# A transformer block with cross-attention on one core: the same instructions of the cross-attention stage in another order on all five engines

## The reference

```python
attn_in  = _adaln(x, cond, ln1_w, ln1_b, g1_w, g1_b, b1_w, b1_b)
x        = _attn(attn_in, attn_in, sa_wq, sa_wkv, sa_wo, sa_bo) + x      # self-attention
cross_in = _adaln(x, cond, ln1_w, ln1_b, g1_w, g1_b, b1_w, b1_b)
ctx_n    = _ln(context, ca_lnc_w, ca_lnc_b)
x        = _attn(cross_in, ctx_n, ca_wq, ca_wkv, ca_wo, ca_bo) + x       # cross-attention
ffn_in   = _adaln(x, cond, ln2_w, ln2_b, g2_w, g2_b, b2_w, b2_b)
x        = _gelu(ffn_in @ ff_w1 + ff_b1) @ ff_w2 + ff_b2 + x

def _attn(xq, ctx, wq, wkv, wo, bo):
    q = _rope(_heads(xq @ wq), sq, cq)                 # rotary embedding of queries
    k, v = split(ctx @ wkv); k = _rope(_heads(k), sk, ck)
    a = softmax(q @ k.T * DH ** -0.5)
    return (a @ v) @ wo + bo
```

## Time and profile before

| | us |
|---|---|
| median of 3 runs (lowest, highest) | 1930.57 (1927.43, 1931.12) |
| the profiled execution: its time, and its span | 1934.22, 1932.4 |

### The profile page before, as it was taken

The page is one execution under the profiler, slowest core; times in us unless marked ns, Lnnn a source line. Parts: engine busy times, 40 slices in busy tenths (PEclk is TensorE's granted clock), DMA queues, the critical chain, the costliest instruction groups (busy, mean ns, idle before and its releaser), DMA issues.

```text
span 1932.4 us, 54308 instructions
## 1 busy us (share of the span) xinstructions
PE 1871.5 (97%) x20617; PEld 1422.7 (74%) x20617; DVE 1480.6 (77%) x2316; ACT 978.1 (51%) x1732; POOL 1306.7 (68%) x859
## 2 busy tenths in 40 slices
PE   7999999978999999999999999999999999999999
PEld 4666767757777777777777777777777777777764
DVE  4999989966777777777777777777777777777741
ACT  3455555534655555455445545545554455445444
POOL 4878756514877777677777766777777678777661
PEclk8999999978999999999999999999999999999999
DMA  5332233211111111111111111111111111111100
GB/s 175 116 87 87 86 103 89 79 33 47 52 54 47 52 49 47 55 49 52 50 49 49 47 51 51 47 54 52 49 47 49 52 53 48 52 49 47 53 26 22
DMA packets 159899, 113.84 MB, mean 59 GB/s; under 512 B 80928, under 2 KB 123808, under 8 KB 159648
## 3 DMA queue, kind: packets, MB, share of 16 engines
q1 hardware_dynamic: 122784, 110.09, 17.5%
q10 hardware_dynamic: 36864, 0.28, 1.0%
HBM read 31.21 MB, written 1.05 MB: 17 GB/s over the span
## 4 chain that ended last, share of the span: by engine, by line
PE 81%; DVE 5%; issue 5%; DMA 4%; POOL 3%; ACT 1%; SPq 1%; ACTq 0%; DVEq 0%; POOLq 0%
PE S L1602 22%; PE OB L1616 19%; PE PB L1513 9%; PE PB L1518 7%; PE S L1583 6%; DMA swapped<-turned 3%; PE S L1385 2%; PE PB L1351 1%; PE S L1636 1%; PE S L1645 1%; PE S L1474 1%; PE S L1627 1%; PE OB L1413 1%; PE OB L1396 1%; POOL psum_acc L769 1%
## 5 line engine op out<-in xcount | busy, mean ns | idle before, releaser
L825 POOL TENSOR_TENSOR psum_acc<-psum_acc,P 124x1024 f32<-124x1024 f32 x256 | 611.3, 2388 | 117.1 <-ACT P L1002 97.8
L1002 ACT ACTIVATE P<-S 124x1024 f32<-124x1024 f32 (+1 forms) x448 | 432.7, 966 | 416.3 <-PE S L1602 416.0
L1223 DVE TENSOR_REDUCE mxc<-S 128x2 f32<-128x1024 f32 x384 | 470.1, 1224 | 152.4 <-PE S L1583 148.3
L1518 PE MATMUL PB<-wsplit,ctxH 64*124 64x256 f32 x1632 | 309.3, 279 | 0.0
L1602 PE MATMUL S<-QH,KH 64*124 64x256 f32 (+1 forms) x1664 | 299.9, 307 | 8.7 <-ACT P L1002 6.1
L1513 PE MATMUL PB<-ctxH,wsplit 64*128 64x512 f32 x1004 | 298.1, 376 | 3.3 <-issue 2.3
L1616 PE MATMUL OB<-P,V 124*64 124x256 f32 (+1 forms) x2236 | 296.3, 389 | 0.0
L1602 PE MATMUL S<-MX,share 64*124 64x256 f32 (+1 forms) x1664 | 275.6, 279 | 0.0
L1602 PE MATMUL S<-QL,KH 64*124 64x256 f32 (+1 forms) x1664 | 275.1, 278 | 0.0
L1602 PE MATMUL S<-QH,KL 64*124 64x256 f32 (+1 forms) x1664 | 275.0, 278 | 0.0
L1602 PEld LDWEIGHTS S<-QH,KH 64*124 64x124 f32 (+1 forms) x1664 | 206.6, 181 | 85.5 <-issue 61.3
(11 more groups left out here) (192 smaller groups left out, 4078.3 us busy)
## 6 DMA issues: line engine op xcount, KB each, us to landing
swapped<-turned SPq DMA_DIRECT2D x512, 128.0 KB, 2.0
kv_w<-sa_kv_dram SPq DMA_DIRECT2D x64, 128.0 KB, 2.3
qswapped<-qturned SPq DMA_DIRECT2D x128, 64.0 KB, 1.9
ctxT_all<-ctx_dram SPq DMA_DIRECT2D x8, 624.0 KB, 4.6
q_w<-sa_wq_dram SPq DMA_DIRECT2D x64, 64.0 KB, 2.0
q_w<-ca_wq_dram SPq DMA_DIRECT2D x64, 64.0 KB, 2.1
o_room<-ca_wo_dram SPq DMA_DIRECT2D x64, 64.0 KB, 2.1
swapped<-turned SPq DMA_DIRECT2D x128, 16.2 KB, 1.8
```

The source lines that it names most:

```text
L825: pool.tensor_tensor(acc, acc, P_of(J, c)[0:rows, :, 0:w], ALU.add).then_inc(x.acc, 1)
L1002: act.activation(P_of(J, c)[0:rows, :, 0:w], SP[0:rows, :, 0:w], ACT.Exp, scale=SCALE).then_inc(x.e, 1)
L1223: dve.tensor_reduce(mxc[:, t, :, c:c + 1], MP[:, :, 0:w], AX.X, ALU.max).then_inc(x.am, 1)
L1518: last_v = pe.matmul(out, context, weights, start=(not second and k == 0), stop=(second and k == len(values) - 1))
```

## The change

The instructions stay the same; their order changes on each engine. The diff of the two lines that show the notation (PE's first, and SP's):

```diff
@@ CROSS = Cross("ca", DC, M, 124, 512,
-                  "s4+-1 x0+1 a5 y0+1 s5+-1 a6 p3+-1 o+-2 p4+-1 s6+-1 x1+1 a0+1 y1+1 s0 n0 p5+-1 a1+1 n1 x2+1 s1 y2+1 a2+1  "
...
-                  "wo+1 k2+1 k3+1 w+4 i+-1 k0+2 q+2 r+5 k1+2")
+                  "s4+-1 x0+1 a5 y0+1 s5+-1 a6 p3+-1 p4+-1 o+-2 s6+-1 x1+1 a0+1 n0 y1+1 s0 a1+1 p5+-1 x2+1 n1 s1 y2+1 a2+1  "
...
+                  "k2+1 wo+2 r+5 k3+1 i+-1 w+4 k0+2 q+2 k1+2")
```

## The result

The kernel after takes 1940.66 us (median of 5 runs, 1938.58 to 1946.6), the kernel before 1930.57 (median of 5, 1927.43 to 1934.46): ratio 1.0058, with a 95% interval of 1.0035 to 1.0080 (a ratio here is made of all runs and isn't the quotient of the two medians). A second set of 11 runs of after gave 1.0032 (1.0017 to 1.0047). By the medians it is slower by 10.1 us in the first set and by 6.9 in the second; forecast were 9.7. Both profiled executions of after are shorter than their medians: 1939.39 us with a span of 1937.6, and a span of 1934.6.

The account below looks back on a forecast made before the run. The prediction took PE, busy 97% of the span, to bound the kernel. Its terms 5.9 + 3.3 + 1.3 - 0.8 gave +9.7 us, 1940.3 us on the median 1930.6, with a range of 1924 to 1949.

Parts of the forecast that it names:

- the main term: On DVE: with `ka3` ahead of `kl2`, late K copies delay PE's `x3`; 5.9 us plus 3.3 for copies covered today.
- Two of its own signs: If right, `x3` waits for `kl2` in ten to eighteen steps; if wrong, late copies are fewer than nine.
- `ka0` before `dv`: On DVE: if `ka0`'s copy is late `dv` waits too, but is due only at `o`; 0 us (-3 to +3).
- `a1` ahead of `p5`: On PE: `a1` would wait for `am0` after late chunk 1 copies, one step in ten; 1.3 us, 0 to 4.
- The tail: Last steps on PE: the mean `n0`, moved ahead of `s0`, fills an idle 0.78 us; -0.8 us.
- SP, ACT, POOL at 0: New orders on SP, ACT and POOL hold nothing up; 0 us, for ACT and POOL 0 to 2.
- its likeliest case: The forecast itself, chance 0.56: 1934 to 1947 us, from no covered late copies and no `a1` wait to both upper bounds.
- The rival of no change: K copies come sooner or meet fewer instruction loads, so the sum goes to about zero: 1931 us; chance 0.20.
- The rival of a faster kernel: In odd steps `am1` and `a2` come 0.3 us sooner with `a1` moved up: 9.3 us, total 1920.5; chance 0.17.
- The clock rival: PE's holes of 1.5 us in nine steps lower its clock to half: 14.5 us more, 1955 us; chance 0.07.

Follow-up runs that it names:

- a_sp: The kernel after with SP's string of before (`wo` ahead of `k2`, `w` right behind `k3`, `r` after `q`): ratio 1.0041 to before.
- a_all3: The kernel after with three edits undone (`kl2` ahead of `ka3`, `dv` ahead of `ka0`, `p5` ahead of `a1`): ratio 1.0002 to before.
- b_ka0: The kernel before with one edit alone, VectorE's `ka0` ahead of `dv`: ratio 1.0061 to before.
- b_pe: The kernel before with TensorE's string of after, except that `p5` stays ahead of `a1`: ratio 0.9995 to before.
- b_ka3: The kernel before with one edit alone, VectorE's `ka3` ahead of `kl2`: ratio 1.0067 to before.

## Why the prediction was right, and where only its sum was

**Right: what bounds it and what carries the loss.** PE does; quiet steps stayed as long within 0.1 us a pair; what counts is which late copies PE gets to feel. In all 14 traces, every single copy of K or Q and of the maxima that was late by over 0.4 us lay beside a load of instructions. The reverse holds too: of 840 copies of chunk 3, 243 had no load that began between 1.5 us before their issue and 3.5 behind it, and each of them landed within 0.02 us of the median. And the mechanism of the main term is in the rows: 1.50 us idle before `x3` where 1.5 was worked out.

**Wrong: the main term, +9.2 us, measured -1.** The step that failed is the count, late copies of the last chunk in 0.29 of the steps (17 or 18), taken over from before to after. That average may serve for a load that falls anywhere. But before, 20 and 23 of 59 were late, and after 7: the same change that made each cost more made them three times rarer. Alone on the old order the edit costs 13.2 us at its place, more than forecast; in the change it costs next to nothing. The prediction had named this as its first rival (loads fall elsewhere as words move), with 0.20, and expected the total to go to zero with it. Two of its own signs speak against the main term: `x3` waits in four and seven steps of the two traces, not in ten to eighteen, and the late copies are seven, fewer than nine.

**Wrong: `ka0` before `dv`, priced at 0 (-3 to +3 for all the rest of DVE), measured +3.9 at `a5` and more with it.** The sentence was "`dv` is due at `o`, behind `p4` now". It looked at who needs `dv`'s result, and not at who needs the room that `dv` reads. `a3`'s wait for `qc` had shown exactly such a wait, in the earlier trace rows, and the same function makes both.

**Too small: `a1` ahead of `p5`, +1.3, measured +4.0.** The price of one such step was nearly right (0.4 us by the starts, 6.8 us in 16 steps; 0.3 forecast). The number of steps was not: the forecast took one in ten, six of 60, and 16 and 11 were late. Chunk 1's late copies had risen from 15 to 22.

**The tail, -0.8, measured +1.5.** The hole was filled and 0.55 us were gained up to the next one. The clock took it back in these two traces, which says nothing of the change, since it does so as often with the old order.

**SP, ACT, POOL at 0:** `a_sp` and `a_all3`, which keeps the new ACT and POOL strings, bear it out. `MX` waits went down by some 1 us (the column `s6` to `s0`), which was not forecast.

So the forecast's 9.7 = 9.2 + 1.3 - 0.8 came out as -1 at `x3`, +3.9 at `a5`, +4.0 at `a1`, -1.1 at `s0`, some 2.4 in quiet steps (0.08 us a pair, 30 pairs) and +1.5 in the tail, 9.7 again. That the two sums meet is luck, and the last term is not the change's. Of these 9.7 the two pairs of spans show 5.2 and 5.8 us (1937.6 - 1932.4, 1934.6 - 1928.8), because the first of the 60 steps began 5.5 and 3.4 us sooner in the traces of after. Of that some 2.8 us lie ahead of the stage's first `q`, and 1.7 in its first three steps, which the table leaves out. It began as early in `b_ka0` and `b_pe`, and late in `a_sp` (474.4 us). Whether an edit is behind that, no run settles. The medians of the runs show 10.1 and 6.9. The sum is right by two couplings of the same kind that took the place of the one that was priced. The range held it for a better reason: it was wide for the number of late copies. (By its own terms its likeliest case reaches from 1936 to 1946, not from 1934 to 1947: 5.9 - 0.8 on one side, 5.9 + 6.4 + 4 - 0.8 on the other.)

**The rivals.** The rival of no change came true in its cause, fewer late copies of chunk 3, but not in the total. Its own sum was off as well: nine steps at 0.3 in place of 0.87 us, +1.3 and -0.8 give -4.6, some 1926 and not 1931. The rival of a faster kernel is refuted: `s2` waits for `e1` as forecast, and the quiet odd step got longer by some 0.06 us. What the page "Perfetto Trace Analysis" of the Trainium skill (section "Identifying the Most-Contended Engine") was taken to mean for order, room by the 74% of weight loads, has no support here: none of the eleven other orders made a quiet step shorter by more than 0.05 us. The clock rival is refuted for the stage of after, where no trace leaves 1.00, but not as a mechanism: it came twice in `b_ka3`. The window right behind the hole of 1.50 us:

```profile
1357.00:1360.00 3.00, 2.41 (x28) 2.16 (x29) 2.31 (x6) 0.56 (x3) 1.04 (x1) 1.00 0.03 0
```

## What to carry to other kernels

When an instruction moves behind one that waits for a DMA, list not only who takes its result but also who overwrites what it reads: in a kernel with shared PSUM rooms the second list is the shorter wait. How many DMAs are late goes with a whole program's order here, and can be counted in a trace, but not carried over to the next order; so price a coupling by its worst count, not its mean, and judge an edit at its place in the step rather than by a total that moves by some us on its own. And a total that fits is no proof of its terms: here the forecast and the time of the first set of runs agree within 1 us, with the largest term off by ten.

## What the runs showed of the hardware

Loads of instructions share the DMA engines with the copies and delay them. The rows are the copies of chunk 3 (16.2 KB each, two to a chunk) with one load near. In 14 traces all 97 with a 16 KB load (q8) that began 0.2 to 2.0 us behind their issue landed late, by 0.5 to 2.1 us. All 18 with an 8 KB load (q14) that began 1.5 to 1.7 us behind it were late by 0.3 to 0.7 us, and two with one that began 0.3 and 1.0 us behind it by nothing. A load that begins earlier or later than that mostly costs nothing, though four with a load at 2.3 to 2.4 us came 2 us late. The page "DMA: Bandwidth & Descriptors" of the Trainium skill (section "Queues, rings and completion order") has each DMA engine take its queues in turn by packets, and these rows agree with it. The loads don't fall evenly: in before, 32 of 189 begin 21 to 23 us behind a `q`, where a load meets chunk 3's copy; in after 9 do. In the second traces it is 30 and 11.

The granted clock of TensorE fell to 1.2 GHz for 3.4 us behind idle times of 1.36 and 1.45 us in `b_ka3`, and stayed at 1.00 behind idle times of 1.44, 1.46 and 1.66 us of the same trace and of 1.50 us in after. Behind the hole of 2.44 us in the tail it fell in every trace, for 3.4 to 13.7 us.
